# Row look-ups, scatters, row sums and turning matmuls of a graph kernel in two halves of 64 weight columns

## The reference

```python
for l in range(3):
    f1 = relu(x[row] @ nb_W[l] + nb_b[l]); f2 = relu(x[col] @ self_W[l] + self_b[l])
    h = relu(concatenate([f1, f2], axis=1) @ att1_W[l] + att1_b[l])
    log_alpha = (h @ att2_W[l] + att2_b[l])[:, 0]
    mask = clip(sigmoid(log_alpha) * (ZETA - GAMMA) + GAMMA, 0.0, 1.0)
    rowsum = segment_sum(mask, row) + 1e-06
    d_inv_sqrt = clip(rowsum ** (-0.5), 0.0, 10.0)
    vals = mask * d_inv_sqrt[row] * d_inv_sqrt[col]
    x = segment_sum(vals[:, None] * x[col], row)
    out = out + x
```

## Time and profile before

| | us |
|---|---|
| time before, median of 3 runs | 11346.42 (11342.84 to 11346.77) |
| span of the profiled execution | 10215.4 |
| first layer's edge stage in the span, about | 1273 to 3065 |
| edge stages of layers two and three, each about | 1190 |
| segment stages, four, each about | 1040 |

### The profile page before, as it was taken

One profiled execution on the slowest core, in us unless ns is written; L12 is line 12 of the kernel. 1 busy time (PEld: TensorE's weight loads), 2 busy tenths in 40 slices (PEclk: granted clock), 3 DMA queues, 4 the chain that ended last, 5 costly groups with the idle time before them and its releaser, 6 DMA issues. The chain is left out here.

```text
span 10215.4 us, 720231 instructions
## 1 busy us (share of the span) xinstructions
PE 8439.0 (83%) x288671; PEld 7571.9 (74%) x288671; DVE 8039.4 (79%) x13908; ACT 3166.6 (31%) x6110; POOL 4364.3 (43%) x4880
## 2 busy tenths in 40 slices
PE   0113288888887999899997999899997999879996
PEld 0112177877776888799997888799997888768885
DVE  9998488888887777777777777777777777777775
ACT  0110156666663333300002333300001333333332
POOL 0002601111116888311114888521112888758883
PEclk9755599999998999999998999999998999989996
DMA  1001277777765555577775555467775555545552
GB/s 27 0 0 27 49 226 232 230 230 232 229 216 143 162 161 160 142 212 214 211 212 155 161 159 161 130 205 212 212 214 170 161 161 160 141 130 160 159 161 70
DMA packets 1005301, 1633.48 MB, mean 160 GB/s; under 512 B 260439, under 2 KB 743635, under 8 KB 1004831
## 3 DMA queue, kind: packets, MB, share of 16 engines
q1 hardware_dynamic: 954104, 1581.29, 52.8%
q0 software_dynamic: 51104, 50.97, 2.3%
HBM read 1345.54 MB, written 286.24 MB: 160 GB/s over the span
## 5 line engine op out<-in xcount | busy, mean ns | idle before, releaser
L1034 PE MATMUL bank<-tab,extra 128*64 128x64 bf16 x201684 | 3981.3, 197 | 389.0 <-DMA extra<-one_hots 230.4
L1034 PEld LDWEIGHTS bank<-tab,extra 128*64 128x64 fp8e4 x201684 | 3566.3, 112 | 877.4 <-issue 817.2
L739 POOL TENSOR_TENSOR planes<-planes 128x448 f32<-128x448 f32 (+1 forms) x2744 | 2610.2, 963 | 542.5 <-DVE planes L1767 476.1
L888 ACT CAST bank<-planes 128x448 f32<-128x448 bf16 (+1 forms) x2744 | 1515.1, 552 | 2289.5 <-DVE planes L1760 2283.0
L1142 PE MATMUL bank<-planes,extra 128*128 128x192 bf16 x19992 | 2098.2, 247 | 43.1 <-POOL planes L739 10.0
L669 POOL DMA_INDIRECT xg<-q_table,ixb x588 | 561.1, 954 | 3592.0 <-ACT ixb L837 3486.3
L1760 DVE TENSOR_TENSOR planes<-bank,mask_all 128x448 f32<-128x448 f32 (+2 forms) x2744 | 1699.0, 619 | 274.2 <-PE bank L1034 171.0
L1767 DVE TENSOR_TENSOR planes<-planes,bank 128x448 f32<-128x448 f32 (+1 forms) x2744 | 1727.4, 630 | 126.5 <-ACT bank L888 126.4
L1142 PEld LDWEIGHTS bank<-planes,extra 128*128 128x128 fp8e4 x19992 | 1584.2, 96 | 172.7 <-issue 55.0
L1640 DVE SCALAR_TENSOR_TENSOR extra<-bank,a2w 128x448 f32<-128x448 f32 (+1 forms) x2058 | 1300.2, 640 | 510.2 <-PE bank L1059 453.7
L1059 PE MATMUL bank<-plb,extra 128*128 128x64 bf16 x44982 | 1595.9, 194 | 14.4 <-ACT plb L869 9.0
(11 more groups left out here) (227 smaller groups left out, 4734.3 us busy)
## 6 DMA issues: line engine op xcount, KB each, us to landing
extra<-one_hots SPq DMA_DIRECT2D x1372, 368.0 KB, 3.3
extra<-one_hots SPq DMA_DIRECT2D x2156, 224.0 KB, 3.6
extra<-one_hots SPq DMA_DIRECT2D x588, 192.0 KB, 2.4
one_hots<-extra SPq DMA_DIRECT2D x490, 224.0 KB, 2.3
one_hots<-extra SPq DMA_DIRECT2D x294, 368.0 KB, 3.9
work<-slot_rows_cols SPq DMA_DIRECT2D x196, 368.0 KB, 5.2
work<-slot_rows_cols SPq DMA_DIRECT2D x294, 224.0 KB, 4.0
work<-slot_rows_cols SPq DMA_DIRECT2D x98, 192.0 KB
```

Source lines behind the costliest of these rows:

```text
L739: nc.gpsimd.tensor_tensor(tiles(yrl[:, 2, a * C:b * C]), tiles(yrl[:, 1, a * C:b * C]), upper[:, 1, a:b, :], ALU.subtract).then_inc(low_re ...
L888: nc.scalar.copy(tiles(z_banks[g][:, 0:(b - a) * C]), upper[:, 0, a:b, :]).then_inc(high_ps, 1)
L1034: mm = pe.matmul(bank[half * S:(half + 1) * S, i * C:(i + 1) * C], oct_[:, k * P + half * S:k * P + (half + 1) * S], tab[:, at:at + C], st ...
```

## The change

Each of the four kinds of matmul is issued twice, with weight columns 0 to 63 and 64 to 127 of the tile, into the lower and the upper half of the output's partitions. The streamed operand is the same for both. Column look-ups are as they were.

```diff
@@ -924,6 +924,7 @@
 
         @block.tensor
         def _(pe):
+            SIDES = (0, S)
             pe.sem_inc(xT_ps, 2)
             pe.sem_inc(f_ps, 2)
             pe.sem_inc(pq_ps, 2)
@@ -1056,8 +1057,9 @@
                     bank = bank_of(g, first)
                     for i, k in enumerate(GROUPS[g]):
                         for pl in range(NPL):
-                            mm = pe.matmul(bank[:, i * C:(i + 1) * C], ort[:, k * P:(k + 1) * P],
-                                           plb[:, pl * C:(pl + 1) * C], start=False, stop=True, skip_group_check=True)
+                            for lo in SIDES:
+                                mm = pe.matmul(bank[lo:lo + S, i * C:(i + 1) * C], ort[:, k * P + lo:k * P + lo + S],
+                                               plb[:, pl * C:(pl + 1) * C], start=False, stop=True, skip_group_check=True)
                     mm.then_inc(z_ps, 1)
 
                 def turn(t, j):
@@ -1068,8 +1070,10 @@
                         wait_alone(pe, or_done, t + 1)
                     k, n = TURNS[j]
                     for i in range(n):
-                        mm = pe.matmul(turn_to(j)[:, i * P:(i + 1) * P], ort[:, (k + i) * P:(k + i + 1) * P], ident_bf,
-                                       start=True, stop=True, skip_group_check=True)
+                        for lo in SIDES:
+                            mm = pe.matmul(turn_to(j)[lo:lo + S, i * P:(i + 1) * P],
+                                           ort[:, (k + i) * P + lo:(k + i) * P + lo + S], ident_bf,
+                                           start=True, stop=True, skip_group_check=True)
                     mm.then_inc(turn_one_hots, 1)
 
                 def row_sums(n, t):
@@ -1081,8 +1085,9 @@
                         for i in range(3):
                             wait_alone(pe, or_in[i], (t - NB) * 16 + 16)
                     for k in range(TT):
-                        mm = pe.matmul(sum_bank[:, 0:NPL + 1], orr[:, k * P:(k + 1) * P], mk_upper[:, k, :],
-                                       start=(k == 0), stop=(k == TT - 1), skip_group_check=first)
+                        for lo in SIDES:
+                            mm = pe.matmul(sum_bank[lo:lo + S, 0:NPL + 1], orr[:, k * P + lo:k * P + lo + S], mk_upper[:, k, :],
+                                           start=(k == 0), stop=(k == TT - 1), skip_group_check=first)
                     mm.then_inc(rs_ps, 1)
 
                 def table_part(g, late):
@@ -1139,8 +1144,9 @@
                         wait_alone(pe, or_in[FIRST_OF[g]], (t - NB) * 16 + 16)
                     wait_alone(pe, low_ready, m * NG + g + 1)
                     for k in GROUPS[g]:
-                        mm = pe.matmul(sum_bank[:, 0:NPL * C], orr[:, k * P:(k + 1) * P], upper[:, :, k, :],
-                                       start=(k == 0), stop=(k == TT - 1))
+                        for lo in SIDES:
+                            mm = pe.matmul(sum_bank[lo:lo + S, 0:NPL * C], orr[:, k * P + lo:k * P + lo + S], upper[:, :, k, :],
+                                           start=(k == 0), stop=(k == TT - 1))
                     mm.then_inc(sc_ps, 1)
 
                 BEFORE = ((3,), (4, 5), (6,), (), (), (), ())
```

## The result

The change takes 12186.91 us (median of 4 runs, 12144.4 to 12199.02) where the kernel before takes 11344.63 beside it: ratio 1.0736, 95% interval 1.072 to 1.0752, 842 us slower. The forecast was 10927 us in a range of 10760 to 11500. The profiled execution took 12144.4 us, its span 12142.7: nothing lies around the span.

What follows compares the result with a forecast made beforehand. TensorE, 83% busy, was taken as the bound, losing time where 64- and 128-column matmuls alternate. Terms -75 (later edges), -314 (segments) and -30 (first layer) sum to -419: 11346 - 419 = 10927 us, range 10760 to 11500.

Steps and rivals of the forecast that it cites:

- rival 1: First layer's 804-matmul loop no longer stays on TensorE and is refetched each pass: +689, 11616 us; chance 0.22 in full.
- all eight blocks or one over: First layer's TensorE loop: 2048 instructions held, refilled 256 at a time, so the longer body just fits or just doesn't.
- each of 97 passes is like the first: First layer's loop, if refetched: every pass loses 4.85 x 804/549 = 7.1 us, +689 us.
- thousands of packets: Sign of refetching in the first layer's loop: what the code queue would show, against 57 packets before.
- 1131 us above it: Whole kernel: runs' median 11346.42 us against the profiled span of 10215.4; the difference was left unchanged in the forecast.
- Segments, -314: Four segment stages, 392 blocks: block falls from 10.62 to 9.8 us, -0.8 each; lower end -384.
- rival 3: Segment stages: halved scatters overlap only in part or GpSimd slows, block 10.1 us, +118, 11045 us; chance 0.08.
- GpSimd's wait before group 1: Segment blocks: this 0.98 us wait shrinks to near zero, leaving GpSimd's pass at 9.8 us.
- Later edge stages, -75: Edge stages of layers two and three, 196 blocks: block falls from 11.96 to 11.58 us, -0.38 each; lower end -141.
- the +0.72 of the forecast: Later edge blocks: added cost of halving, +0.38 us for row look-ups and at most +0.34 for row sums.
- the 1.10 us at changes of kind: Edge blocks: ten switches between 64- and 128-column matmuls, 5 x 0.12 + 5 x 0.10 us, vanish.
- First layer, -30: First layer's edge stage, 98 blocks of 17.87 us: -0.3 each, between 0 and -78 in all.

Runs made afterwards that it cites:

- e6: The whole change except that the first layer's turning matmuls stay full, against the kernel before: ratio 0.9992, 70 code packets.
- e2: Only the scatters in halves, all else as in the kernel before: ratio 0.9889, -127 us.
- e14: Only the scatters halved, with plain transfers for the indirect gathers, against the kernel before: ratio 0.9015, 201 us below e13.
- e13: The kernel before with each block's two indirect gathers replaced by plain transfers: ratio 0.9193, 908 us less.
- e9: e6 with a one-column matmul ahead of each turning matmul, again 804 matmuls in the loop: ratio 1.1629 to the kernel before, 376 code packets.
- e12: The kernel before with two blocks per pass in TensorE's segment loops, scatters halved in one of the two: ratio 0.9937.
- e17: The whole change with 77 transposes ahead, moving later TensorE code by 153 instructions: 0.9901, 10122.51 us against 10225.69 for the kernel before.
- e15: The change without halved turning matmuls, with plain transfers for the gathers: ratio 0.9098 to the kernel before, 91 us above e14.
- e16: e6 with 51 extra one-column matmuls of 64 weight columns ahead of the first layer's row sums: ratio 1.0318 to the kernel before, 70 packets.

## Why the prediction was wrong

**The step that failed** is the chance of rival 1: "I give 0.22 to the full miss". The 804-matmul loop was taken to stay on the engine, because "1608 and some 60 waits and register steps fit", and it doesn't stay. The mechanism was named, the place too; the price was 7.1 us a pass and 689 us. Measured beside e6, which has all the rest of the change: (1.0736 - 0.9992) x 11345 = 844 us, 8.7 a pass. The forecast's own sentence "with a body cut by block borders and one block fetched ahead it is all eight blocks or one over" was the right question; counting the built program's instructions up to the loop, and laying the borders through the standstill of the earlier trace rows, would have shown that the loop touches eight pieces. That eight are too many, no row of the kernel before shows. The Trainium skill (Runtime: NRT & Kernel Launch, Instruction fetch mechanics) gives 2048 instructions in 256 at a time, eight pieces; 466 packets with 7.63 MB are 16 KB each, its figure. Here a loop that touches eight is fetched again in most passes and one that touches seven isn't. That the eighth place is taken by a piece fetched ahead fits this, but no run shows it.

The size was off in two ways. That "each of 97 passes is like the first" isn't so: nine packets serve two passes, so not every pass fetches all of its pieces, and the "thousands of packets" were 466. Yet a pass costs more in the mean than forecast. The standstills of the pass in the rows above add up to 13.5 us, and the granted clock is 0.75 in the stage, where it is 0.88 around the pass from which the price was scaled (1290 to 1330 us).

**The baseline.** "1131 us above it, and I leave that part as it is" was false. The traced execution had no stalls beside the gathers, the timed ones had. They are also why the gains of e2 (-127) came out smaller than in e14 (-201). e13 shows that within one session the indirect form of the gathers brings them; why the same kernel has them in some sessions (11240 to 11345 us) and not in another (10226) stays open. It isn't the chip alone: the sessions of e9 to e12 and of e17 were on the same one.

**Segments, -314.** Measured without stalls: -203 from the first block starts to the last of the four stages (traces of before and e17), and -201 in e14. In the rows a block is 10.04 us and not 10.62. The price was right: (1.40 - 0.248)/27 = 42.7 ns a half, 85 a pair for 86.4, so rival 3's dearer scatter fell. What failed is that GpSimd's wait before group 1 goes to near zero and its own 9.8 us then bound the block. A block is a ring through three engines. From TensorE's scatters of group 1 to VectorE's sum it is 7.08 us (9010.36 to 9017.44), from there to GpSimd's group 1 another 1.78, and from there to the next scatters of group 1 another 1.18: together 10.04. In the kernel before the last two were the same, 1.77 and 1.19, by this row:

```profile
9508.91 0.84 PE L1142 MATMUL bank<-planes,extra 128*128 128x192 bf16 x8
```

So TensorE's part was 10.62 - 2.96 = 7.66. The change shortens this part by 0.58 and nothing else of the ring; GpSimd's wait falls from 0.98 to 0.47 and no further. e14 shows the ring closed: TensorE's 0.26 is released by GpSimd, GpSimd's 1.08 by VectorE. The 0.27 before a scatter group in e17 has no releaser in the trace.

**Later edge stages, -75.** Measured +0.51 us in the block of the rows, and +116 from the first starts to the last of both stages. Row look-ups at 15.8 ns a half ((2.16 - 0.196)/124), row sums at 15.9 ((1.78 - 0.171)/101), as taken at the upper bound: the +0.72 of the forecast. Of the 1.10 us at changes of kind some 0.85 went: 42 look-ups from 5418.99 on are followed after 0.69 us instead of 0.80. But three gaps grew that the forecast had put at nothing. At the loop's branch 125 row look-ups (1.99 us at their price) hold 2.53, so 0.54 is lost where it was 0.36. Ahead of the row sums 41 (0.65) hold 0.98, so 0.33 where it was 0.17. And some 0.3 us follow the starts of the two gathers, as at 5413.19, where 48 row look-ups hold 0.87 us; e15, with plain transfers, has 0.77 there and a block of 12.2 us. A stream of halves has less slack: at 15.9 ns for 4 as for 64 streamed elements, what limits it is no longer the stream, so what TensorE must do between matmuls shows. That reason I argue from the rows; no run took the waits away.

**First layer, -30.** Without fetching, +0.05 us in the block of the rows and -8 over the whole stage: next to nothing gained, in a stage where VectorE and ScalarE are waited for.

The three terms by whole stages, without stalls and fetching: +116 - 203 - 8 = -95. The two spans (10215.4 and 10121.1) differ by 94, and e17 gained 103 in time beside the kernel before. The forecast of -419 was four times too large even where its rival doesn't hold; the loss in the later edge stages was in none of the rivals.

**What was right:** the gaps at changes of kind (0.11 us each, e9), the prices of the pairs, and the overlap of alternating halves.

## What to carry to other kernels

Before making a loop's body longer, count the instructions up to its start and its length in the built program, and ask how many pieces of 256 it touches; moving code can be worth more than the change (1.0736 and 0.9901 are the same loops, each beside the kernel before in its own session). Check that the trace is of an execution that took the time that is to be improved; if span and time differ by a tenth, it isn't. And halves pay where a pair costs no more than the full matmul and changes of kind go (the scatters alone, e2: 0.9889, 11215 us, faster than both kernels), not where the full matmul's stream is short (row sums, 25.1 ns to 31.8).

## What the runs showed of the hardware that I hadn't expected

- GpSimd's indirect gather of 128 rows of 256 bytes stalls TensorE's issue, from 0.8 to 1.1 us after its start: up to three times half a microsecond. A plain transfer of the same bytes from the same engine doesn't (11243 to 10334 us), and nor does the gather itself in one session (10226 us) and in the trace of before.
- A loop of 1668 instructions costs 8.7 us a pass more in the mean or nothing, by its place alone. Its packets of 16 KB come as two and seven in turn, the first standstill of every second pass is 5 to 8 us long, and the granted clock behind it is 0.50.
- Two halves alternating: 85 ns for 192 streamed elements; swept by groups, 17 ns more a pair. Halves of 4 streamed elements take the same 15.9 ns as those of 64. Matmuls of one streamed element in the same half, one after another, take 32 (e16).
